# Sharing one gathered tile in every 8 or 12 groups between SyncE and GpSimd, in loops of one ring turn

## The reference

```python
edge_index = jnp.stack([src, dst])
h = relu(layernorm(x))
x = x + layer0(edge_index, h, Wq, Wk, Wv, gamma, beta, 8)
h = relu(layernorm(x))
x = x + layer1(h, cos_beta, edge_index)

def layer0(...):                       # attention with 8 heads
    q, k, v = h[src] @ Wq, h[dst] @ Wk, h[dst] @ Wv
    e = exp(clip(sum(q * k), -10, 10))         # per edge and head
    res = segment_sum(e / (segment_sum(e, src)[src] + 1e-8) * v, src) + h
    return layernorm(res) * gamma + beta

def layer1(...):                       # cosine attention
    a = sum(h[src] * h[dst]) / (norm[src] * norm[dst]) * cos_beta
    a = exp(a - segment_max(a, src)[src])
    return segment_sum(a / segment_sum(a, src)[src] * h[dst], src)
```

## Time and profile before

| what | value |
|---|---|
| median of 3 runs | 7085.51 us |
| the profiled execution | 7131.92 us |
| its span | 7130.1 us |
| stretch of layer 0's groups | about 690 to 3940 us |
| stretch of layer 1's groups | about 4052 to 7070 us |
| DVE busy | 4103.2 us (58%) |
| PE busy | 4342.2 us (61%) |
| POOL busy | 3380.1 us (47%) |
| ACT busy | 2444.7 us (34%) |
| DMA of SP for rows by hand | 3,200 in layer 0, 2,048 in layer 1 |

### The profile page before, as it was taken

How to read it: one execution, slowest core, us unless ns; L and a number is a source line. 1 busy time by engine, 2 the same in 40 slices (tenths; PEclk the granted TensorE clock), 3 DMA queues, 4 the chain that set the end, 5 groups by cost and what they waited for, 6 DMA issues and landing times. The chain is left out here.

```text
span 7130.1 us, 118004 instructions
## 1 busy us (share of the span) xinstructions
PE 4342.2 (61%) x22945; PEld 3749.1 (53%) x22946; DVE 4103.2 (58%) x12176; ACT 2444.7 (34%) x8557; POOL 3380.1 (47%) x3426
## 2 busy tenths in 40 slices
PE   6997555555555555555455156677667676666665
PEld 3886344434443444434344156676666676666665
DVE  8998555555555555555556545555555555555555
ACT  4997111111110111111011544454454444444443
POOL 1334555545454554545454245555555555555552
PEclk8998666666666666666666576666676666776666
DMA  1001222222222222222222112121221121112111
GB/s 35 25 23 34 81 80 76 77 75 77 74 79 77 77 77 75 77 75 79 77 76 73 38 43 48 46 48 47 48 47 47 47 49 46 47 47 49 46 45 39
DMA packets 211652, 414.52 MB, mean 58 GB/s; under 512 B 69399, under 2 KB 103640, under 8 KB 211068
## 3 DMA queue, kind: packets, MB, share of 16 engines
q0 software_dynamic: 135184, 326.41, 17.4%
q1 hardware_dynamic: 74048, 79.04, 3.8%
q10 hardware_dynamic: 1836, 4.03, 0.2%
HBM read 363.52 MB, written 42.48 MB: 57 GB/s over the span
## 5 line engine op out<-in xcount | busy, mean ns | idle before, releaser
L892 POOL DMA_INDIRECT kv_rows<-kv_table,idx_ring x1643 | 1624.6, 989 | 1590.9 <-issue 1003.7
L892 POOL DMA_INDIRECT h_rows<-h_table,idx_ring x1652 | 1566.7, 948 | 1592.7 <-issue 1029.9
L1132 PE MATMUL psum<-vx,hot 128*128 128x136 f32 x3336 | 864.0, 411 | 1135.6 <-DVE acc L1165 1041.0
L1132 PEld LDWEIGHTS psum<-vx,hot 128*128 128x128 f32 x3336 | 696.2, 287 | 1280.3 <-DVE acc L1165 1140.8
L1628 DVE SCALAR_TENSOR_TENSOR h_sb<-h_sb,corr,psum 128x129 f32 x1668 | 582.8, 349 | 931.8 <-PE psum L1586 496.4
L1165 DVE TENSOR_TENSOR acc<-acc,psum 128x136 f32 x1668 | 489.4, 293 | 1006.2 <-remote 850.0
L1576 PE MATMUL psum<-ident,hotl 128*128 128x128 f32 x1668 | 393.9, 381 | 952.7 <-DVE highs L1654 880.6
L1080 ACT ACTIVATE vx<-clip 128x32 f32<-128x32 f32 x417 | 95.2, 229 | 2332.1 <-DVE clip L1209 1878.7
L1576 PEld LDWEIGHTS psum<-ident,hotl 128*128 128x128 f32 x1668 | 258.5, 192 | 1030.6 <-issue 895.4
L1121 PE MATMUL psum<-q_sb,hotT 128*128 x3336 | 712.0, 380 | 32.9 <-issue 23.0
L1121 PEld LDWEIGHTS psum<-q_sb,hotT 128*128 128x128 f32 x3336 | 607.5, 273 | 184.7 <-issue 184.7
(11 more groups left out here) (225 smaller groups left out, 5834.1 us busy)
## 6 DMA issues: line engine op xcount, KB each, us to landing
hand<-kv_table SPq DMA_DIRECT2D x3200, 1.0 KB
hand<-h_table SPq DMA_DIRECT2D x2048, 0.5 KB
own_rows<-own SPq DMA_DIRECT2D x104, 256.0 KB
own<-own_rows SPq DMA_DIRECT2D x104, 256.0 KB
h_rows<-h_table,idx_ring POOLq DMA_INDIRECT x1652
kv_rows<-kv_table,idx_ring POOLq DMA_INDIRECT x1643
kv_table<-kv SPq DMA_DIRECT2D x21, 256.0 KB, 2.1
out<-q_sb SPq DMA_DIRECT2D x2, 1536.0 KB
```

The costliest lines, as they stand in the source:

```text
L892: pool.indirect_dma_start(out=G[:, k, j, :], out_offset=None, in_=table, in_offset=bass.IndirectOffsetOnAxis(ap=idx[:, k, j:j + 1], axis=0 ...
L1132: last = nc.tensor.matmul(S_ps[j // HALF][:, j % HALF, :], hot[:, k, j * P:(j + 1) * P], vx[:, k, j, :], start=True, stop=True)
```

## The change

The tile by hand is split. In every turn of the ring (8 groups in layer 0, 12 in layer 1) POOL gathers slots 0 to 63 of the last tile of the last group with an indirect DMA of 64 rows, and SP fetches slots 64 to 127 one by one; ACT copies 64 partitions from `hand` to `G`, at step 5 of 8 in layer 0 and step 10 of 12 in layer 1. The bodies of all loops hold one turn. SP still issues 8 rows behind each group of layer 0, and 6 behind each of 11 of 12 groups of layer 1. The sharing begins with the second turn, so there are 51 shared tiles in layer 0 (TURNS0) and 33 in layer 1 (TURNS1). Layer 0's row numbers for SP are now read from `names` in HBM, behind eight stores into it, where two DMAs read them from SBUF beside four stores.

```diff
+FROM0, FROM1 = 64, 64
+BYHAND0 = (P - FROM0) // RING0
+COPY0_AT = 5
+BYHAND1, HAND1_AT, COPY1_AT = 6, 10, 10
+TURNS0, TURNS1 = (GROUPS - RING0) // RING0, (GROUPS - RING1) // RING1
...
+def shared(u, t, ring):
+
+    return u == ring - 1 and not (isinstance(t, int) and t == 0)
...
+        for j in range(GT):
+            n = whole if j == GT - 1 and shared(u, t, ring) else P
+            pool.indirect_dma_start(out=G[0:n, u, j, :], out_offset=None, in_=table,
+                                    in_offset=bass.IndirectOffsetOnAxis(ap=idx[0:n, u, j:j + 1], axis=0)
+                                    ).then_inc(s_gat[u], 16)
+    walk(pool, step, ring, first=0, drain=0)
...
-            per = P // (HAND0 * GT)
-            for h in range(per):
-                q = HAND0 * GT * (h + 1) - 1
-                sp.dma_start(ids.rearrange("o (k h c) -> o k h c", h=per, c=P)[:, :, h, :],
-                             names[q:q + 1, :, :]).then_inc(s_ids, 16)
-            for a in range(4):
+            for a in range(P // ROW):
...
+            sp.wait_ge(s_names, 16 * (P // ROW))
+            sp.dma_start(ids.rearrange("o (n c) -> o n c", c=P - FROM0),
+                         names_of(dram, RING0)[:, :, FROM0:P]).then_inc(s_names, 16)
...
-                for r in range(BYHAND):
-                    p = BYHAND * u + r
-                    sp.dma_start(hand[p:p + 1, :], dram["kv"][ds(named[0][BYHAND * (u % 2) + r], 1), :]
+                for r in range(BYHAND0):
+                    p = FROM0 + BYHAND0 * u + r
+                    sp.dma_start(hand[p:p + 1, :], dram["kv"][ds(named[0][BYHAND0 * (u % 2) + r], 1), :]
...
-            walk(sp, step, HAND0, first=0, drain=0, peel=2)
+            walk(sp, step, RING0, first=0, drain=0, peel=2)
...
+                    indices(i + RING0, u)
+                    if u == COPY0_AT and shared(RING0 - 1, t, RING0) and (not isinstance(t, int) or t <= TURNS0):
+                        for k in range(2):
+                            act.wait_ge(s_hand[k], 16 * (P - FROM0) // 2 * t)
+                        act.wait_ge(s_vx, RING0 * t)
+                        nc.scalar.copy(G[FROM0:P, RING0 - 1, GT - 1, :], hand[FROM0:P, :]).then_inc(s_copied, 1)
+                    keep_own(i + NEAR, (u + NEAR) % RING0, t + (u + NEAR) // RING0)
```

More of the change, by code:

```diff
@@ L74 @@
 QUADS = -(-GROUPS // FOUR)
[L75 to L83, removed]
+FROM0, FROM1 = 64, 64
+BYHAND0 = (P - FROM0) // RING0
+COPY0_AT = 5
+BYHAND1, HAND1_AT, COPY1_AT = 6, 10, 10
+BATCHES1 = -(-(P - FROM1) // BYHAND1)
+EVEN1 = sum(min(BYHAND1, P - FROM1 - BYHAND1 * b) for b in range(0, BATCHES1, 2))
+TURNS0, TURNS1 = (GROUPS - RING0) // RING0, (GROUPS - RING1) // RING1
 PART = 7
@@ L865, in last_words, with gather_groups @@
     return dram["sorted"][WHOLE * P * P:WORDS].rearrange("(q c) -> q c", c=P)
[L868 to L881, removed]
+def shared(u, t, ring):
+    return u == ring - 1 and not (isinstance(t, int) and t == 0)
+def gather_groups(pool, ring, table, G, idx, s_idx, s_read, s_gat, s_go, whole):
     def step(i, u, t):
@@ L885, in step @@
             return
-        k = u % ring
-        hand = period is not None and by_hand(u, t, period)
         pool.wait_ge(s_idx, i + 1)
@@ L890, in step, with names_of @@
         pool.sem_inc(s_go, 1)
[L891 to L895, removed]
+        for j in range(GT):
[4 more added lines that the diff above has]
+    walk(pool, step, ring, first=0, drain=0)
+def names_of(dram, ring):
+    turn = ring * GT // ROW
+    first = (2 * ring * GT - 1) // ROW
+    turns = (GROUPS - ring) // ring
+    rows = dram["names"].rearrange("k a c -> (k a) c")
+    return rows[first:first + turn * (turns - 1) + 1:turn, :].rearrange("(o n) c -> o n c", o=1)
 def own_quad(dram, q, n):
@@ L907, in spread_row @@
     nc.tensor.matmul(out, pick_row[:, g_u % FOUR, :], rows[:, h, :], start=True, stop=True).then_inc(s_spread, 1)
[L910 to L914, removed]
 def layer0_edges(nc, mem, dram):
@@ L1012, in hand_rows @@
             def hand_rows(u, t):
-                if isinstance(t, int) and not 1 <= t < GROUPS // HAND0:
+                if isinstance(t, int) and not 1 <= t <= TURNS0:
                     return
@@ L1081, in step @@
                                          ACT.Exp).then_inc(s_ex, 1)
[L1082 to L1088, removed]
+                    indices(i + RING0, u)
[5 more added lines that the diff above has]
+                    keep_own(i + NEAR, (u + NEAR) % RING0, t + (u + NEAR) // RING0)
             for g in range(NEAR):
                 keep_own(g, g, 0)
-            walk(act, step, HAND0, first=0, drain=0)
+            walk(act, step, RING0, first=0, drain=0)
         @block.tensor
@@ L1213, in step @@
                         add_unit(i, u, t, h)
-            walk(dve, step, HAND0, first=-4, drain=4)
+            walk(dve, step, RING0, first=-4, drain=4)
 def between_layers(nc, mem, dram):
@@ L1455, in hand_rows @@
             def hand_rows(u, t):
-                n, b = (t, u - HAND1_AT) if u >= HAND1_AT else (t - 1, u + HAND1 - HAND1_AT)
-                if b >= BATCHES1 or isinstance(n, int) and not 1 <= n <= HANDS1:
+                n, b = (t, u - HAND1_AT) if u >= HAND1_AT else (t - 1, u + RING1 - HAND1_AT)
+                if b >= BATCHES1 or isinstance(n, int) and not 1 <= n <= TURNS1:
                     return
@@ L1544, in _ @@
                 widen_own(g, g, 0)
-            walk(act, step, HAND1, first=0, drain=7)
+            walk(act, step, RING1, first=0, drain=7)
         @block.tensor
@@ L1683, in step @@
                     need(dve, s_hotw, i + 1 - RING1)
-                    nc.vector.tensor_tensor(hot[:, u % RING1, :, :], under(loc_b[:, ds(GT * i, GT)], P),
+                    nc.vector.tensor_tensor(hot[:, u, :, :], under(loc_b[:, ds(GT * i, GT)], P),
                                             iota_j[:, :, :], ALU.is_equal).then_inc(s_hot, 1)
-            walk(dve, step, HAND1, first=0, drain=9)
+            walk(dve, step, RING1, first=0, drain=9)
 def finish(nc, mem, out):
@@ L1729, in program @@
         "own": nc.dram_tensor("own_rows", (QUADS, P, FOUR * GE), u8).ap(),
-        "names": nc.dram_tensor("tile_names", (WHOLE, 4, P), i32).ap(),
+        "names": nc.dram_tensor("tile_names", (WHOLE, P // ROW, P), i32).ap(),
         "kv": nc.dram_tensor("kv_table", (NPAD, 2 * D), f32).ap(),
```

79 lines of the change are left out of this document (41 added, 38 removed).

## The result

| | before | after |
|---|---|---|
| median, us | 7094.74 (7075.83 to 7130.73, 4 runs) | 7227.53 (7215.62 to 7242.6, 4 runs) |
| profiled execution, us | 7131.92 | 7237.01 |

The ratio is 1.0182, 95% interval 1.0134 to 1.0231: the change costs 133 us. I forecast 7110, with a range that ended at 7190.

What follows compares the result with a forecast made beforehand. SP's row issue was taken to bound layer 0, POOL's bursts and the chain of DVE, PE and ACT layer 1. Terms 2 + 6 + 5 + 4 + 3 + 5 = +25 us gave 7110 us, range 7020 to 7190.

Steps and rivals of the forecast that it cites:

- What bounds the kernel: SP's row issue, slowed by POOL's bursts, paces layer 0 at 7.73 us per group; SP is no bound in layer 1.
- Hand-over, +2 us: Layer 0, SP's wait for landing and copy: 50 at 1.34 us replace 24 at 2.65 and one at 1.34.
- SP's pace 8 groups earlier, +6: Layer 0: SP fetches from group 8, not 16, so eight groups go from about 7.0 to 7.73 us.
- the start, +3: Start of layer 0: four more stores, two fewer number reads and a DMA that waits for the stores add 3 us.
- The gather of 64 rows, +9 us: POOL's half gather costs 0.77 us against 1.25 for a whole: +5 us in layer 0, +4 in layer 1.
- rival B: POOL, both layers: a half gather costs a whole one; +42 us in place of +9, 7143 us, chance 0.18.
- Loop ends in layer 1, +5 us: DVE's 17 more turns cost at most +36 us, ACT's vanished stalls give at best -32; overlapping, +5 us.
- rival C: DVE's branch sets layer 1's pace: 17 x 2.1 = +36 us in place of +5, 7142 us, chance 0.12.
- rival D: Layer 0: POOL's bursts start anew with each hand-over and lock to the turn; +400 us, about 7500, chance 0.08.
- Rival A: Layer 0: SP stops waiting at the hand-over, if others need over 7.57 us per group; 7043 us, chance 0.22.

Runs made afterwards that it cites:

- the last run above: The kernel before with SP fetching all 128 rows of one tile in 32 groups of layer 0 instead of 16: 6852.12 us, ratio 0.9619.

## Why the prediction was wrong

**What bounds the kernel** held: SP without waits, ACT and DVE behind it, gathers that slow it (the run with extra gathers). The run with 32 rows is the proof that SP's rows hold layer 0: it falls by 294 us, from 3242 on the same chip. I had the pieces and did not ask what the rows buy.

**Hand-over, +2 us**: held in each part. 3.38 us at a turn's end was forecast as 3.3, SP's wait is 1.0 us each, and putting the longer loop back costs 51 us. ACT waits 15 us at a copy, not 10. By the rule of the Trainium skill ("Runtime: NRT & Kernel Launch", Instruction fetch mechanics) a taken branch stalls when its target is not in the two blocks of 256 instructions that the engine holds. The trace agrees as far as it goes: SP's body, 218 instructions, does not stall, and DVE's of layer 1, 416, does, although 416 are fewer than two full blocks; no run was made to vary where a body lies in its blocks.

**SP's pace 8 groups earlier, +6, and the start, +3**: the first product comes 1.3 us later, where the start's term had 3. No run tests the 6; both are small.

**The gather of 64 rows, +9 us, was mis-sized: this step failed.** I halved the 0.94 us and got 0.77 us per gather. It takes 0.91, so each occupies POOL almost as long as a whole one: rival B. My 0.30 us fixed were the pause between two gathers, and I had no row that showed how much of the 0.94 was fixed. With 0.8 to 1.4 us on the path of layer 0 and 0.1 to 1.0 in layer 1, the 25 and 16 more come to 20 to 35 and 2 to 16 us. The Trainium skill's "small, variable" ("DMA: Bandwidth & Descriptors", Anatomy of one DMA, SWDGE) was nearer than my half: the trace has 0.04 us for 64 rows.

**Loop ends in layer 1, +5 us, failed too:** rival C came, at 28 us by the medians and some 60 in the profiled executions, where I had 36 at most. Two steps of the term failed. I charged 2.1 us per branch, the 3.98 less an ordinary wait of 1.9; DVE idles 4.2 us behind each, and with 17 branches fewer its idle time there fell by 79 us. And I set ACT's lost stalls against DVE's new ones: ACT's did go (0.2 us from its branch to the next instruction, where it was 2.5), but layer 1 still grew. The reserve in POOL's ring did not absorb DVE's stalls, except on the chip of 6992 us. Layer 1 took over 3035 us, the mark I had set for C.

**The sum.** Layer 0: 2 + 6 + 3 + (20 to 35) = 31 to 46, measured 47 (in the repeated profiles on one chip 72). Layer 1: (2 to 16) + (28 to 60) = 30 to 76, measured 68. What is missing in layer 0 shows as rows issued more slowly: the bursts now come as 12, 12 and 8 gathers in nearly every turn (parted by pauses of over 1 us, 102 of 12 and 48 of 8 among 154 in the trace of POOL; before 81 of 12, 27 of 4, 21 of 8 and 14 of 15 among 157), the locking that rival D feared, at a small part of its price. That this is the cause was argued, not tested.

**The range** took B and C together as +89 over the forecast's terms and ended at 7190. Both came, and layer 0's rest on top put it at 7228. The probabilities treated B and C as alternatives; they were independent and happened together.

**Rival A** fell at its condition: it needed the others to take over 7.57 us per group, and layer 0 passes at 7.1 to 7.2 without SP's hold. So ACT reached the copy first, as before, and SP's 64 rows and hand-over, 8 x 7.83 = 62.6 us, set the length of each turn.

## What to carry to other kernels

Before you split a transfer, find out whether its price lies in its rows or in its issue: half a gather at the price of a whole one makes the other half's work a pure addition. When work has been moved off one engine to relieve it, measure what the receiving engine is the bound of; taking the help away or halving it is a one-constant experiment, and here it was worth some 240 us. And count how often each engine's loop branches: here the shorter body helped SP, whose body fell from 432 to 218 instructions and stopped stalling, and cost DVE in layer 1, whose body of 416 still stalls and now branches 17 times more.

## What the runs showed of the hardware that I had not expected

- A gather of 64 rows holds POOL 0.91 us, one of 128 0.95 us.
- Under a burst of gathers it is not SP's DMAs alone that slow down. In the trace of the changed kernel from 2052 to 2062 us, SP's register moves and register loads, too, stand some 0.7 us apart, singly or in twos and threes, where a move takes 0.03 us in a pause of POOL. The cause stays open.
- Loop bodies of 213 to 241 instructions (SP, DVE, ACT) had about 0.2 us from a branch to the next instruction, bodies of 416 to 458 had 2.4 to 3.3 us in the median, and SP's body of 476, in the last run above, 0.7 us (0.0 to 2.2). With DVE's stall a register load at the body's head, 1.10 us, is exposed as well.
- Taking SP's rows out of layer 1 made that layer 100 us longer at the same number of gathers, in two runs, and fetching them for nothing gave most of it back. The cause stays open.
- One chip ran the kernel before in 6992 us, the others in 7095 to 7121, and single parts scaled differently there: layer 0 of the changed form 3116 us against 3223 to 3262, and DVE's branch stalls, as long in the trace, without effect on layer 1.
